# Attention score maxima laid out for neighbouring queries, and an even-bank seed put between two exponentials

## Reference

```python
qkv = X @ W_qkv                                   # 16 heads of 64, X layer-normed
scores = einsum('bqhd,bkhd->bhqk', q, k) / 8
weights = softmax(scores, axis=-1)
attn = einsum('bhqk,bkhd->bqhd', weights, v)      # then @ W_out
```

## Time and profile before

| | us |
|---|---|
| median of 3 runs (lowest, highest) | 1887.1 (1886.76, 1893.81) |
| profiled execution | 1889.88 |
| its span, first to last instruction | 1888.0 |
| of it, from the copy that ends piece 0 to the one that ends piece 31 | 1356.1 (31 pieces, 43.75 each) |

### The profile page before, as it was taken

How to read it: one execution, slowest core, us unless ns; L and a number is a source line. 1 busy time by engine, 2 the same in 40 slices (tenths; PEclk the granted TensorE clock), 3 DMA queues, 4 the chain that set the end, 5 groups by cost and what they waited for, 6 DMA issues and landing times. The chain is left out here.

```text
span 1888.0 us, 32039 instructions
## 1 busy us (share of the span) xinstructions
PE 1785.0 (95%) x9247; PEld 989.1 (52%) x9247; DVE 1519.8 (80%) x2053; ACT 1464.2 (78%) x1954; POOL 1448.2 (77%) x868
## 2 busy tenths in 40 slices
PE   5799999999999999999999999999999899985687
PEld 4445444454454455554544544545445587763456
DVE  6787788888878777878878888778788788888896
ACT  4388888888888888888888888888888688874653
POOL 4288888888888888888888888888888457755564
PEclk9899999999999999999999999999999999997899
DMA  7112021212121121202121212112121577531000
GB/s 249 60 54 78 34 78 35 78 46 76 45 67 47 66 83 48 78 34 78 35 79 54 68 45 67 54 59 89 41 78 34 174 226 248 154 95 56 0 18 28
DMA packets 117014, 143.31 MB, mean 76 GB/s; under 512 B 18417, under 2 KB 98353, under 8 KB 113778
## 3 DMA queue, kind: packets, MB, share of 16 engines
q1 hardware_dynamic: 111986, 132.61, 22.4%
q0 software_dynamic: 4992, 10.27, 1.6%
HBM read 87.20 MB, written 27.64 MB: 61 GB/s over the span
## 5 line engine op out<-in xcount | busy, mean ns | idle before, releaser
L1530 POOL TENSOR_TENSOR psum_k<-psum_k,probs 128x1024 f32<-128x1024 f32 x384 | 929.9, 2422 | 144.8 <-ACT probs L1471 125.8
L1549 DVE TENSOR_REDUCE mxh<-ps_m 128x2 f32<-128x1024 f32 x518 | 623.6, 1204 | 242.7 <-PE ps_m L1285 242.6
L1471 ACT ACTIVATE probs<-ps_s 128x1024 f32<-128x1024 f32 x512 | 496.9, 1023 | 164.0 <-PE ps_s L1301 146.3
L1310 PE MATMUL ps_v<-probs,V 128*64 128x512 f32 x2056 | 494.6, 602 | 0.0
L1310 PEld LDWEIGHTS ps_v<-probs,V 128*64 128x64 f32 x2056 | 130.5, 136 | 239.2 <-issue 183.8
L1455 ACT ACTIVATE ps_s<-qkv_raw 128x1024 f32<-128x1024 f32 x224 | 243.6, 1124 | 0.0
L1455 ACT ACTIVATE ps_s<-peak 128x1024 f32<-128x1024 f32 x224 | 243.6, 1122 | 0.0
L1565 DVE RECIPROCAL e_y_row<-e_y_row 128x128 f32<-128x128 f32 x256 | 241.4, 943 | 0.0
L1530 POOL TENSOR_TENSOR psum_k<-probs 128x1024 f32<-128x1024 f32 x64 | 152.6, 2384 | 63.7 <-ACT probs L1471 47.7
L1301 PE MATMUL ps_s<-e_ew 64*128 64x512 f32 x1536 | 198.8, 390 | 0.0
L1285 PE MATMUL ps_m<-e_ew 64*128 64x512 f32 x524 | 163.9, 622 | 5.4 <-DVE mxh L1549 4.7
(11 more groups left out here) (317 smaller groups left out, 2918.0 us busy)
## 6 DMA issues: line engine op xcount, KB each, us to landing
e_ew<-w_split SPq DMA_DIRECT2D x23, 1024.0 KB
qkv_raw<-peaks SPq DMA_DIRECT2D x33, 512.0 KB, 3.9
V<-e_x_raw SPq DMA_DIRECT2D x33, 512.0 KB, 5.1
peak<-peaks SPq DMA_DIRECT2D x32, 512.0 KB, 4.1
xs_hi<-xh SPq DMA_DIRECT2D x16, 512.0 KB, 4.1
xs_lo<-xl SPq DMA_DIRECT2D x16, 512.0 KB, 5.0
rows<-in_blank_d SPq DMA_DIRECT2D x4, 1483.5 KB, 16.1
e_x_raw<-rows SPq DMA_DIRECT2D x23, 258.0 KB
```

Source lines behind the costliest of these rows:

```text
L1310: ins = nc.tensor.matmul(ps_v[rows, :], V[par][:, kt, rows], probs[:, t % RING, x, :], start=kt == 0, stop=kt == KT - 1)
L1471: nc.scalar.activation(probs[:, t % RING, :, :], ps_s[t % 2][:, :, :], ACT.Exp, scale=SCALE).then_inc(p_done, 1)
L1530: nc.gpsimd.tensor_tensor(acc, probs[:, (t - 1) % RING, :, :] if kt == 1 else acc, probs[:, t % RING, :, :], ALU.add).then_inc(add_done, 1)
L1549: nc.vector.tensor_reduce(mxh[:, kh, t, :], max_bank(unit, i)[:, :, :], AX.X, ALU.max).then_inc(m_done, 1)
```

## The change

Three things, all in `layer0_attention`:

1. Group t of `row_max` takes 128 neighbouring queries (hf * 512 + t * 128 + q on partition q), a contiguous slice of `q_hi` in place of one with a step of 4 elements (16 bytes).
2. So the 8 numbers of a partition are 2 heads x 4 groups (`mx` is [P, 2, 4]), and `peak` comes out as [128 q, 2 heads, 4 groups]. The seeds, which write the score bank in the order head, group, query, read `peak` with a step of 8 elements (32 bytes) in place of 2 elements (8 bytes). What they write, and the bytes that the DMAs move, stay the same in number and form.
3. ACT writes the seed of the even step t + 2 straight behind E, ahead of O; before, it stood behind the item's read. It writes into the bank that E has just read, and waits on `p_done` for E's end (it did before, where O and the copy stood between the two). The count of instructions on each engine is unchanged.

```diff
--- before.py
+++ after.py
@@ -47,7 +47,7 @@
     g.psum_k = [sb(f"psum_k{h}", [P, 2, CH], F32) for h in range(2)]
     g.place = sb("place", [P, 2, TILES], U32)
     g.ones = sb("ones", [P, DH], F32)
-    g.mx = sb("mx", [P, 4, 2], F32)
+    g.mx = sb("mx", [P, 2, 4], F32)
     g.V = [sb(f"V{p}", [P, TPB, 2 * DH], F32) for p in range(2)]
 
     spare = g.psum_k[0][:, :, :].rearrange("p x c -> p (x c)")
@@ -1003,7 +1003,8 @@
     w_in, preset, w_staged, wlo_staged, add_done = g.attn_w_in, g.preset, g.w_staged, g.wlo_staged, g.add_done
     even = [w[:, k * T:(k + 1) * T] for w in g.w_first for k in range(2)]
     k_hi, k_lo, q_hi, q_lo = ([even[k], sb(f"{name}1", [P, T], F32R)] for k, name in enumerate(("k_hi", "k_lo", "q_hi", "q_lo")))
-    peak = [qkv[:, 2, :, :].rearrange("p a d -> p (a d)").rearrange("p (c x) -> p c x", x=2), sb("peak1", [P, CH, 2], F32)]
+    peak = [qkv[:, 2, :, :].rearrange("p a d -> p (a d)").rearrange("p (q x t) -> p x t q", x=2, t=4),
+            sb("peak1", [P, P, 2, 4], F32)[:, :, :, :].rearrange("p q x t -> p x t q")]
     V_next = g.V_next
     xs_hi = sb("xs_hi", [P, T], F32R)
     xs_lo = sb("xs_lo", [P, T], F32R)
@@ -1138,6 +1139,9 @@
     def chunk(name):
         return slice(int(name[1]) * CH, (int(name[1]) + 1) * CH)
 
+    def scores_of(tile):
+        return tile[:, :, :].rearrange("p x (t q) -> p x t q", t=4)
+
     def pairs(eng):
 
         with eng.Fori(0, N // 2) as i:
@@ -1166,9 +1170,9 @@
             def spread(unit, hf):
 
                 sp.wait_ge(mx_done, unit + 1)
-                sp.dma_start(g.peaks[hf:hf + 1, :].rearrange("a (q k) -> q (a k)", k=8), mx[:, :, :].rearrange("p t x -> p (t x)")).then_inc(mx_out, 16)
+                sp.dma_start(g.peaks[hf:hf + 1, :].rearrange("a (q k) -> q (a k)", k=8), mx[:, :, :].rearrange("p x t -> p (x t)")).then_inc(mx_out, 16)
                 sp.wait_ge(mx_out, unit * 16 + 16)
-                sp.dma_start(peak[hf][:, :, :].rearrange("p c x -> p (c x)"), g.peaks[hf:hf + 1, :].to_broadcast([P, 2 * CH])).then_inc(peak_in, 16)
+                sp.dma_start(peak[hf].rearrange("p x t q -> p (q x t)"), g.peaks[hf:hf + 1, :].to_broadcast([P, 2 * CH])).then_inc(peak_in, 16)
 
             load_part(0)
             spread(0, 0)
@@ -1280,9 +1284,9 @@
                         pe.wait_ge(m_done, unit * KT + i - 1)
                 else:
                     pe.wait_ge(m_done, unit * KT + i)
-                q = q_hi[par][:, :].rearrange("p (c t) -> p t c", t=4)[:, t, hf * P:(hf + 1) * P]
+                q = hf * CH + t * P
                 for x, rows in enumerate(HEADS):
-                    ins = nc.tensor.matmul(m[:, x, :], q[rows, :], k_hi[par][rows, kh * CH:(kh + 1) * CH],
+                    ins = nc.tensor.matmul(m[:, x, :], q_hi[par][rows, q:q + P], k_hi[par][rows, kh * CH:(kh + 1) * CH],
                                            start=True, stop=True)
                 ins.then_inc(m_ready, 1)
 
@@ -1452,14 +1456,14 @@
                 if t % KT < 2:
                     act.wait_ge(peak_in, peaks_of(n, t))
                 act.wait_ge(p_done, P0 + n * STEPS + t - 1)
-                nc.scalar.activation(ps_s[t % 2][:, :, :], peak[hf][:, :, :].rearrange("p c x -> p x c"), ACT.Copy, scale=-1.0).then_inc(seeded, 1)
+                nc.scalar.activation(scores_of(ps_s[t % 2]), peak[hf], ACT.Copy, scale=-1.0).then_inc(seeded, 1)
 
             act.wait_ge(preset, LATE_PRESETS)
             act.wait_ge(routed, 2)
             act.wait_ge(armed, 1)
             act.wait_ge(peak_in, 16)
             for k in range(2):
-                nc.scalar.activation(ps_s[k][:, :, :], peak[0][:, :, :].rearrange("p c x -> p x c"), ACT.Copy, scale=-1.0).then_inc(seeded, 1)
+                nc.scalar.activation(scores_of(ps_s[k]), peak[0], ACT.Copy, scale=-1.0).then_inc(seeded, 1)
             for n, par in pairs(act):
                 for t in range(STEPS):
                     p = t // 2
@@ -1470,12 +1474,12 @@
                         act.wait_ge(add_done, ADD0 + n * 2 * ADDS + added(t + STEPS - RING) - 2 * ADDS)
                     nc.scalar.activation(probs[:, t % RING, :, :], ps_s[t % 2][:, :, :], ACT.Exp, scale=SCALE).then_inc(p_done, 1)
                     if t % 2 == 0:
+                        seed(n, t + 2)
                         continue
                     for name in VISIT[p][:1]:
                         read(n, name, par if name == "K0" else 1 - par)
-                    for k in (t + 1, t + 2):
-                        if k not in BY_V:
-                            seed(n, k)
+                    if t + 2 not in BY_V:
+                        seed(n, t + 2)
                     if p == 0:
                         keep_values(n * 2 + 1)
                         expert_part(n)
@@ -1551,7 +1555,7 @@
                     v.wait_ge(m_done, unit * KT + KT)
                     if not (isinstance(unit, int) and unit == 0):
                         v.wait_ge(mx_out, unit * 16)
-                    nc.vector.tensor_reduce(mx[:, :, :], mxh[:, :, :, :].rearrange("p k t x -> p t x k"), AX.X, ALU.max).then_inc(mx_done, 1)
+                    nc.vector.tensor_reduce(mx[:, :, :], mxh[:, :, :, :].rearrange("p k t x -> p x t k"), AX.X, ALU.max).then_inc(mx_done, 1)
 
             def low(n, name, par):
                 hi, lo = (k_hi, k_lo) if name[0] == "K" else (q_hi, q_lo)
@@ -1678,7 +1682,7 @@
 
                 v.wait_ge(p_done, P0 + n * STEPS + t - 1)
                 v.wait_ge(peak_in, peaks_of(n, t))
-                nc.vector.tensor_scalar(ps_s[t % 2][:, :, :], peak[t // KT][:, :, :].rearrange("p c x -> p x c"), -1.0, None, ALU.mult).then_inc(seeded_v, 1)
+                nc.vector.tensor_scalar(scores_of(ps_s[t % 2]), peak[t // KT], -1.0, None, ALU.mult).then_inc(seeded_v, 1)
 
             for n, par in pairs(v):
                 nxt = 1 - par
```

## The result

| | before | after |
|---|---|---|
| median of 4 runs (lowest, highest), us | 1888.84 (1886.76, 1893.81) | 2235.23 (2234.68, 2238.54) |
| ratio, 95% interval | | 1.183 (1.181 to 1.186) |
| span of the profiled execution, us | 1888.0 | 2236.7 |
| a piece, mean over 31, us | 43.75 | 54.59 |

The change makes the kernel 346 us slower. 31 pieces take 10.84 us more each, 336 of the 348.7 us by which the span grew. Forecast was 2182, 53 us too low. The windows of the changed kernel, with the columns of the earlier trace rows: all 31 pieces, then visits 2, 3 and 6 of one piece.

The account below looks back on a forecast made before the run. PE with the one reduction between its two row_max was taken as the bound before, ACT after in ordinary visits. Visits summed to 52.98 us against 43.75: 9.23 more, times 32 = 295 us, giving 2182; range 1940 to 2240.

Parts of the forecast that it names:

- Part 1: PE's row_max weight load falls from 305 to 188 ns: 60 us gained if PE's loop stays the bound.
- s: Extra time of an ACT seed reading with a 32-byte step: 0.85 us, bounds 0, 0.62 and 0.94.
- Wait from E to the seed: On ACT, the even seed starts 0.12 us after E's end, bounds 0 and 0.25.
- Denominators 0.05 us behind low: In visits 1 and 4, PE's denominators load at 5.42, low ending at 5.37; 7.92 us for each visit.
- Visits 0 and 6, PE's loop: With one ACT seed in these visits, PE's loop decides their length: 5.25 us each.
- the 0.06 for a handover: In visits 0 and 6, a term of 0.06 us within the 5.25 us of PE's loop.
- The clock: In the changed profile, PE idle 1.2 us in a visit might get a clock below 1.00, adding time; no size given.
- Step costs nothing: Rival listed first: ACT's seeds cost no more (s = 0), only the order adds, +70 us: 1957 us; chance 0.13.
- Faster: Rival: PE's loads get short and nothing else shows, -60 us, 1827 us; chance 0.06.
- No change: Rival: s is small and the loads' 60 us just pay for the order; chance 0.05.
- the load stays at 305: Rival: PE's weight load is not shortened; main case grows 0.12 in four visits, 15 us; no chance of its own.

Follow-up runs that it names:

- pairs_late: The kernel before with queries paired: row_max loads step 8 bytes, seeds read two neighbouring numbers every 32 bytes, both seeds behind the copy as before; 1842.84 us, ratio 0.975.
- after_short_adds: The changed kernel with GpSimd's additions of steps 9, 14 and 15 cut to 64 of 512 columns; 2240.06 us, ratio 1.179.
- pairs_early: The same as pairs_late but with the even seed between E and O; 2014.71 us, ratio 1.069 to the kernel before.
- one-input `tensor_scalar`: Form of normalise with one SBUF input, division left out; put into order_only it took 2016.17 us, ratio 1.067, into the changed kernel 2234.00 us, 1.182.
- order_only: The kernel before with only the even seed moved between E and O, queries and seed reads as before; 2026.22 us, ratio 1.069.

## Why the prediction was right, and where its size was off

The mechanism held: ACT becomes the bound through seeds that read with a step of 32 bytes. Its forecast was +295 us (9.23 a piece), measured +10.84 a piece. By its own steps:

- **Part 1, the load 305 to 188 ns: right** (191). That it is worth nothing once ACT is the bound, and much if PE stays it, is also right: `pairs_late` keeps it and gains 44 us where 60 were forecast.
- **Seed 1.97 us, s = 0.85: right rule, low price.** Measured 2.10, s = 0.98, outside the upper bound of 0.94. PE's and DVE's rows gave 1.64 to 1.73 ns an element; it is 1.86. DVE's seed likewise 2.13 for 1.84: its extra of 156 ns per 256 elements came from an instruction of another form (two inputs, one of them in PSUM), and that it would carry over was assumed.
- **Wait from E to the seed, 0.12: measured 0.03.** Together with O's 0.90 us (0.97 forecast) this hid the former error in visit 2, and turned visits 1 and 5 slightly under the forecast (7.83 for 7.92, 6.72 for 6.88).
- **Denominators 0.05 us behind low, visits 1 and 4 alike: 0.12, and not alike.** Visit 4 is 8.13 because ACT's copy of the values waits for normalise. With short additions it is 7.79.
- **Visits 0 and 6, PE's loop, 5.25 each: 5.01 and 5.02 when nothing else interferes**, 0.24 below the forecast. In visit 6 the odd row_max starts 0.66 us after E and the next E comes 1.32 us after the even row_max, both as forecast; but between the two row_max lie 3.04 us and not 3.21, and the 0.06 for a handover is not there. In fact visit 0 takes 6.00, since normalise now stands for most of GpSimd's addition. The prediction had the row of normalise's place in visit 7, used it in the first rival at 0.82 us, and never asked what else ran beside it: even those 0.82 us hold a wait for an addition. This is a missing term: 0.99 in visit 0 and 0.34 in visit 4.
- **The clock** stood in the last paragraph as a sign of being wrong and as what would add to the time, with no number. The sign came: the loop's clock is 0.97. It is in 13 of 27 pieces in visit 6 (6.61 for 5.02 us) and in 16 in visit 3 (6.87 for 6.58). (13 x 1.59 + 16 x 0.29) / 27 = 0.94 us a piece at most, 30 us; a little of it comes back in visit 7, which is shorter behind such a visit 6.

The missing term and the clock are 1.33 + 0.94 = 2.27 us. Visits 1, 4 and 5 and PE's loop in visits 0 and 6 came in 0.86 lower than forecast, visits 3 and 7 0.21 higher, which gives the miss of 1.61 us a piece (52 us) to 0.01. So the forecast's closeness owes something to errors of both signs. The two terms are not independent either: in `after_short_adds` one went away and the other grew.

**The rivals.** *Step costs nothing*: refuted by the groups of the seeds. Its pricing of the order is refuted too: 1957 forecast, where `pairs_early`, the kernel that it describes, has a ratio of 1.069, about 2019 on the same scale. Its largest item outside visits 1 and 4, 0.75 us in visit 7, stands in visit 0 instead and is 3.1 us there. *Faster*: the gain of the loads is there, but only with pairs. *No change*, and *the load stays at 305*: refuted by the rows.

**Open.** What about PE's idle time makes the clock fall in visit 6 of one piece and visit 3 of the next is not settled, only that less idle time made it rarer, and that its price could not be measured apart from the visits that it replaces. In which mode the one-input `tensor_scalar` ran is not shown. Why layout and order don't add is argued only.

## What to carry to other kernels

Before changing the layout of a small tensor, list each of its readers and price the inner step of each: to save 0.117 us on 16 loads a piece, this change paid 0.98 us on 14 seeds. Often a third layout serves both, here groups of two neighbours (8-byte step for one reader, pairs for the other), 2.5% faster than before. When a step is moved by about 2 us, look not only at who waits for it, but at what then runs beside it: the worst part of the new order was an instruction pushed from the end of another engine's to the start of its next one.

## What the hardware showed that I had not expected

- ACT's price for a step is a cliff between 8 and 16 bytes: 1138 to 2049 ns for 1024 numbers, and from there to 128 bytes flat (1916 to 2097). DVE has the same: 1217 to 2019 at 16 bytes. Two neighbours every 32 bytes cost ACT 1133.
- A DMA of 128 x 32 bytes to DRAM took 1.3 us and one of 1024 x 4 bytes 10.0, as SyncE waited for it.
- Normalise, 682 ns by itself, took 2.53 us in the mean in visit 7 of `order_only`, beside a GpSimd addition. In every run with whole additions it ended 0.55 us behind one (0.28 in the one-input form), however early it started. Its 0.82 us in the kernel before are such a wait too, a short one.
- An engine that gets faster or waits less need not shorten the kernel if another's idle time lowers PE's clock: 1.33 us a piece won in two visits left 0.18.
